# Who copies the values' rows out of PSUM: VectorE behind the keys' maxima, or ScalarE behind their exponentials

## The reference

```
x = x + gnn(xn, edge_attr, src, dst) + mix(xn)          # mix: 4 layers
x = x + ffn(layernorm(x))                                # 16 experts, 2 chosen per node
```

```
q = softmax(split(h @ Wq) * scale, axis=-1)
k = softmax(split(h @ Wk) * scale, axis=-2)              # over the 3125 rows
v = split(h @ Wv)
context = einsum('bhnd,bhne->bhde', k, v)
out = einsum('bhnd,bhde->bhne', q, context) @ Wo + bo
```

## Time and profile before

| what | value |
|---|---|
| median of 3 runs | 2426.01 us (2425.75 to 2429.09) |
| the profiled execution: its time | 2427.93 us |
| the profiled execution: its span | 2426.2 us |
| TensorE matmul busy | 2035.1 us (84%) |
| VectorE busy | 1542.0 us (64%) |
| GpSimd busy | 1365.6 us (56%) |
| ScalarE busy | 951.4 us (39%) |

### The profile page before, as it was taken

One profiled execution on the slowest core, in us unless ns is written; L12 is line 12 of the kernel. 1 busy time (PEld: TensorE's weight loads), 2 busy tenths in 40 slices (PEclk: granted clock), 3 DMA queues, 4 the chain that ended last, 5 costly groups with the idle time before them and its releaser, 6 DMA issues. The chain is left out here.

```text
span 2426.2 us, 36176 instructions
## 1 busy us (share of the span) xinstructions
PE 2035.1 (84%) x10736; PEld 1661.2 (68%) x10736; DVE 1542.0 (64%) x3503; ACT 951.4 (39%) x1978; POOL 1365.6 (56%) x1118
## 2 busy tenths in 40 slices
PE   2359899998989999898999998899999775699990
PEld 2248677777767777776777777777777564688880
DVE  4658777666876767687777667866766456511116
ACT  1234444443544444443444444444444242133330
POOL 4156666667556666665666666566666400366650
PEclk7769999999999999999999999999999786799995
DMA  8652222224222223332322224222222432599997
GB/s 200 187 136 67 73 67 67 67 67 122 64 71 67 69 72 72 96 83 73 72 67 68 68 71 111 68 66 68 67 71 67 88 96 85 181 302 305 306 289 165
DMA packets 269614, 266.96 MB, mean 110 GB/s; under 512 B 146079, under 2 KB 203510, under 8 KB 269526
## 3 DMA queue, kind: packets, MB, share of 16 engines
q0 software_dynamic: 127488, 134.76, 23.2%
q1 hardware_dynamic: 137926, 131.35, 18.6%
q10 hardware_dynamic: 4112, 0.03, 0.1%
HBM read 229.85 MB, written 35.06 MB: 109 GB/s over the span
## 5 line engine op out<-in xcount | busy, mean ns | idle before, releaser
L780 POOL DMA_INDIRECT G<-P_d,src_T x896 | 1159.2, 1294 | 708.4 <-DVE z L419 428.7
L387 ACT ACTIVATE zr<-z 125x512 fp32r<-125x512 f32 x448 | 275.0, 631 | 551.3 <-DVE z L419 507.9
L419 DVE TENSOR_TENSOR z<-bank,G 125x512 f32<-125x512 f32 x448 | 293.4, 686 | 226.9 <-PE bank L379 96.4
L1190 PE MATMUL bank<-TT,W_s 128*128 128x250 f32 (+1 forms) x1280 | 369.3, 439 | 1.0 <-ACT TT L838 0.9
L1057 PE MATMUL bank<-W_s,hid 128*125 128x256 f32 x1600 | 359.6, 379 | 0.0
L1057 PEld LDWEIGHTS bank<-W_s,hid 128*125 128x125 f32 x1600 | 292.8, 187 | 42.8
L1190 PEld LDWEIGHTS bank<-TT,W_s 128*128 128x128 f32 x1280 | 242.7, 196 | 104.3 <-issue 12.1
L393 DVE SCALAR_TENSOR_TENSOR zl<-z,zr 125x512 fp32r<-125x512 f32 x448 | 288.4, 684 | 8.1 <-ACT zr L387 8.1
L371 PE MATMUL bank<-zr,onehot 125*125 125x256 f32 x896 | 271.3, 334 | 12.8 <-DVE zl L393 12.8
L372 PE MATMUL bank<-zl,onehot 125*125 125x256 f32 x896 | 230.3, 288 | 0.0
L922 ACT ACTIVATE hid<-bank,b1c 128x375 f32<-128x375 f32 x320 | 163.0, 521 | 100.1 <-PE bank L1190 90.5
(11 more groups left out here) (310 smaller groups left out, 3103.4 us busy)
## 6 DMA issues: line engine op xcount, KB each, us to landing
W_s<-in_L_ffn_w SPq DMA_DIRECT2D x64, 512.0 KB
hid<-in_L_ffn_w SPq DMA_DIRECT2D x64, 512.0 KB
G<-P_d,src_T POOLq DMA_INDIRECT x896
W_s<-in_L_mix_W SPq DMA_DIRECT2D x8, 1024.0 KB
aT<-attr_d SPq DMA_DIRECT2D x224, 31.2 KB
attr_d<-hn SPq DMA_DIRECT2D x12, 246.1 KB, 3.7
X<-in_x SPq DMA_DIRECT2D x5, 560.0 KB
P_d<-es SPq DMA_DIRECT2D x25, 112.0 KB
```

What stands on the lines that cost most here:

```text
L387: nc.scalar.activation(zr[:, s, k, :], z[:, k, :], ACT.Relu).then_inc(r_done, 1)
L419: nc.vector.tensor_tensor(z[:, k, :], edge_bank[k][0:ET, :], G[:, ST * s + 2 * k:ST * s + 2 * k + 2, :].rearrange("p j d -> p (j d)"), ALU ...
L780: pool.indirect_dma_start(G[:, j, :], None, P_d[:, :], bass.IndirectOffsetOnAxis(ap=src_T[:, at:at + 1], axis=0)).then_inc(g_in[j], 16)
L1190: ins = pe.matmul(to[:, 0:(b - a) * T], W1_s[:, k, part], TT[:, k, TT_PIECES[pc]], start=k == 0, stop=k == KD - 1)
```

## The change

The three copies of the values' rows leave VectorE's program and enter ScalarE's. There they stand behind the two exponentials of their piece: slots 0 and 1 behind those of piece 0, slot 2 behind those of piece 1. They increment the same semaphore `row_dve` as before, and since VectorE also increments it (for the context's update), each copy now waits for its own number in `row_dve` too. Nothing else differs.

```diff
@@ ScalarE, the first pass of a layer @@
                     u0, q0 = l * RING_L + g * RING_GA + (RING_A + LNU), l * (2 * NG) + g * 2
+                    r0 = l * ROW_L + g * ROW_GA + ROW_A
                     for pc, (a, b) in enumerate(PC):
                         act.wait_ge(cd_done, q0 + pc + 1)
                         act.activation(corr[:, pc, :], cdiff[:, pc, :], ACT.Exp).then_inc(corr_done, 1)
                         for h in range(KD):
                             act.activation(eT[:, h, a * T:b * T], RING[(2 * pc + h) % 3][:, 0:(b - a) * T], ACT.Exp,
                                            bias=nb[:, pc, h:h + 1], scale=SCALE).then_inc(ring_act, 1)
+                        for i in ((0, 1), (2,))[pc]:
+                            c, d = RP[i]
+                            act.wait_ge(row_full, r0 + i + 1)
+                            act.wait_ge(row_dve, r0 + i + 1)
+                            act.activation(V5[:, c:d, :, 0:128].rearrange("p j k n -> p (j k) n"),
+                                           ROW[i % 2][0:T, 0:(d - c) * D].rearrange("p (k n) -> p k n", n=128), ACT.Copy).then_inc(row_dve, 1)
                     normalised(u0 + 4, 4)
@@ VectorE, first(g, after) @@
                         dve.tensor_copy(mO[:, :], mN[:, :]).then_inc(m_cp, 1)
-                        for i in ((0, 1), (2,))[pc]:
-                            c, d = RP[i]
-                            dve.wait_ge(row_full, r0 + i + 1)
-                            dve.tensor_copy(V5[:, c:d, :, 0:128].rearrange("p j k n -> p (j k) n"),
-                                            ROW[i % 2][0:T, 0:(d - c) * D].rearrange("p (k n) -> p k n", n=128)).then_inc(row_dve, 1)
                     edges(eg, eg, 0)
```

## The result

Over 13 runs of each, the changed kernel took 2439.12 us (median) and the kernel before 2429.93 us. The two medians lie 9.2 us apart. The ratio over all runs is 1.0034 with a 95% interval of 1.0023 to 1.0044: slower, by 8.3 us (5.6 to 10.7). The forecast was slower by 6.5 us. The forecast was set on the first three of the 13 runs of the kernel before, and the median of all 13 lies 3.9 us above theirs. So its 2432.5 us is to be read as a shift of 6.5, which lies inside the interval. Added to the forecast's 2426.01 us, the measured shift gives 2434.3 us, inside the range of 2428.5 to 2438.5; the 2439.12 us themselves lie 0.6 us above it. The changed kernel, measured again beside later experiments, gave 1.0025 (1.0013 to 1.0036), 6.1 us.

The account below looks back on a forecast made before the run. The prediction took a circle of waits between ScalarE, TensorE and VectorE to bound each group. Sixteen regular groups of 0.31 us and four first groups of 0.38 us add 6.5 us to 2426.01: 2432.5 us, range 2428.5 to 2438.5.

Parts of the forecast that it names:

- The circle: Chain of waits through a 17.00 us regular group, said to set its length; none of VectorE's three copies is in it.
- VectorE's relief: VectorE loses 35.8 us of busy time, costed at nothing: waits of 0.43 us (K3's maximum) and 1.09 us (z) cover it.
- Piece 0: ScalarE's copies behind piece 0's exponentials: TensorE's loads for slot 2 come 0.04 us late, costing nothing that lasts.
- Piece 1, the term that counts: Third copy between last exponential and first TT: 0.50 us step, 0.19 us covered, 0.31 us shift a regular group.
- The first groups: A layer's first group: bank freed 0.21 us late, slot 2 late with it, first TT 0.38 us later.
- The sum: 16 regular groups of 0.31 us and 4 first groups of 0.38 us make 6.5 us: 2432.5 us.
- In series: ScalarE's copy overlaps neither neighbour, or ROW[0] comes so late that slot 2 is late; 2439.4 us; 8 in 100.
- Hidden: Slack behind the first TT takes up the delay, or the copy is short; 2426 to 2429 us; 15 in 100.
- VectorE was the limit: z's start depends on VectorE finishing its third copy; -7.6 us, 2418.4 us; 5 in 100.
- rival E: Repeated run's rival: change costs about 0.5 us a layer at the lower TensorE clock, 2 us or more outside first passes.

Follow-up runs that it names:

- e5: The changed kernel with the third copy executed twice on ScalarE, first into a free buffer; measured +12.6 us (9.2 to 16.0) against the kernel before.
- e6: The kernel before with ScalarE taking the first two es copies between the two zr; measured -1.0 us (-3.2 to 1.2) against it.
- e4: The kernel before with VectorE's three copies cut to one column, values left out of the context; measured +2.4 us (0.2 to 4.4) against it.
- e2: The kernel before with only the copies of slots 0 and 1 moved to ScalarE; measured +0.7 us (-2.2 to 3.4) against it.
- e3: The changed kernel with the third copy placed behind the five es copies on ScalarE; measured +3.6 us (1.5 to 5.8) against the kernel before.
- e1: The kernel before with only the third copy moved to ScalarE, behind piece 1's exponentials; measured +4.9 us (1.7 to 7.8) against it.
- e10: e9 with all three copies on VectorE, slots 0 and 1 behind the normalisations; measured -6.1 us (-8.7 to -3.4) against the kernel before.
- e9: e6 plus zl before the one-hot matrix, hn behind piece 0's update, slots 0 and 1 copied on ScalarE; 2418.02 us, ratio 0.9941 to the kernel before.
- e7: e6 with all three copies on ScalarE, the third behind the es copies; measured -0.2 us (-2.7 to 2.2) against the kernel before.

## Why the prediction was right

**The circle.** It named last exponential, first `TT`, N7, edges' product, z, `zr`, `es`, transposes, context, next keys. e5 shows it at its sharpest: 0.48 us put between the last exponential and the first `TT` make the group 0.49 longer. e6 shows the other end: removing the wait for `es` shortens it.

**VectorE's relief costs at nothing.** Right for this order of the work: e4 takes the copies away without giving them to anyone, and the groups move by 0.01 us. The covers were those named, with 0.42 us left before K3's maximum.

**Piece 0.** A regular group's loads for slot 2 were forecast 0.04 us late, and the rows by form show 1.1 us of such waiting in all, over 20 groups. Right that it doesn't last. In e2 the first groups show 0.10 us of it, which the prediction had only as a part of its 0.38.

**Piece 1, the term that counts.** The start of the copy was forecast at 8.86 us behind the first keys and was there; its duration at 588 ns and measured 597; the start of `TT` at 9.36 us and measured 9.34, because the copy moves the next instruction by 0.48 and not 0.50 us. So 0.29 us a group in place of 0.31. The Trainium skill's cycle count (VectorE: DVE Perf Modes, on the TRN2 errata) gives an estimate of 570 ns for 512 columns. The trace's 597 ns are 27 above it, as the 378 ns for 256 were 21 above; the rows of the trace were the better base. (The 5.8 us that the prediction gives for this price come out at 5.6 with its own overlap of 0.11 us: four times 0.32 and sixteen times 0.27.)

**The first groups.** Forecast 0.38, measured 0.28 us. The step was too dear: I let the 0.21 us of lateness of ROW[0] pass in full to slot 2. TensorE's loads did wait 0.23 us, but the matmuls behind them started 7.84 us behind the first keys as before, since the loads run ahead of the matmuls (in the kernel before they start 0.21 us earlier, at 7.63). N4 came 0.11 us later and the copy at 9.89 us instead of 9.97.

**The sum.** 5.8 us by the groups, 6.5 forecast, 8.3 and 6.1 measured. That the forecast lies so near the second measurement and inside the first one's interval is in part luck: the groups are what it was about, and there it was 0.7 us too high. The traces show where differences arise outside the first passes. Behind the last layer's context the kernel before took 865.8 us to the end of the span, the changed one 872.4, the same changed kernel again 869.0, e2 863.4 and e4 873.9, though all five execute the same instructions there. Over the thirteen comparisons of the table, measured less groups goes from -3.0 to +3.4 us with both signs, so I take the 2.5 us of the first measurement for scatter of the rest; that is argued, not shown. For e3 and e4 the groups' figure lies outside the measured interval, so some of the rest is more than noise of the measurement there. What it is stays open; no run isolates it.

**The rivals.** *In series*: every pair overlapped, and nothing of it came. *Hidden*: excluded by e1, where the third copy alone makes the groups 0.29 us longer, and by e5. *VectorE was the limit*: excluded by e4 for this kernel. The Trainium skill (Perfetto Trace Analysis, on optimizing Scalar and DVE operations) says that offloading from a saturated VectorE may make sense. In this order of the work the trace disagrees; in another it agrees, since between e10 and e9 it is worth 0.18 us a regular group. VectorE's busy share doesn't tell the two apart: 14.43 us of 17.00 in the kernel before, 14.61 of 16.72 in a group of e10. In these runs the sign was whether K3's maximum has to wait for TensorE: it does, by 0.42 us, where the relief was worth nothing, and doesn't in e10.

## What to carry to other kernels

Where engines run in fixed orders, follow the waits around one period of the loop and note each engine's slack at the place where work is put in or taken out; an engine at half load can be the one that has none. Moved work costs its start-to-start distance less the wait that stood there (0.48 - 0.19 = 0.29 us in a regular group), and it is worth looking for a later place, ahead of its reader, where the engine would wait anyway (5 us later in e3). In these runs relief on the other engine paid nothing as long as that engine waited for TensorE behind the relieved place, so test a move again after each reordering: the same two copies on ScalarE were worth nothing (e2), cost 0.12 us (e7) and gained 0.18 us (e9 against e10) a regular group in three orders of the same work.

## What the hardware showed that I had not expected

Eight of the queries' matmuls, early in a layer's second pass, run at either level of TensorE's clock, and which one differs from trace to trace. In the third layer they followed an idle time of 2.74 us in the kernel before and of 3.07 us in the changed one; six microseconds from there on had a granted clock of 1.00 (2.4 GHz) and of 0.72, a mixture of that and 1.2 GHz. The windows view of those six microseconds (length; busy us of PE, PEld, DVE, ACT, POOL; PEclk; DMA), of the kernel before and of the changed one:

```profile
1131.30:1137.30 6.00, 4.50 (x22) 3.46 (x22) 3.30 (x5) 1.27 (x1) 4.28 (x4) 1.00 0.33 84
```

```profile
1134.50:1140.50 6.00, 4.86 (x15) 3.59 (x15) 2.14 (x5) 0.82 (x1) 3.72 (x4) 0.72 0.35 85
```

The eight matmuls took 1.99 and 3.64 us. TensorE's timeline, again of the kernel before and then of the changed one:

```profile
1131.33 1.99 PE L1057 MATMUL bank<-Wq_s,TT 128*125 128x256 f32 x8 [2.74 <-DVE qe L1496]
```

```profile
1134.56 3.64 PE L1064 MATMUL bank<-Wq_s,TT 128*125 128x256 f32 x8 [3.07 <-DVE qe L1498]
```

Over the four layers these eight matmuls took 2.72, 1.99, 1.99 and 1.99 us in the kernel before, 3.64, 1.99, 3.64 and 1.99 in the changed one, and 3.40, 1.99, 3.65 and 2.47 in the changed one again. That is 2.6 and 2.8 us more in sum than in the kernel before, as rival E of the repeated run would have it. The other traces speak against the change as its cause: e1 and e5, which have the third copy too, took only 1.1 and 0.6 us more than the kernel before, while e2 and e4, whose regular groups are those of the kernel before, took 2.4 and 4.6 us more. Over all fourteen traces the sum goes from 8.0 us (e9) to 13.3 (e4), whose matmuls in the third layer were at the same granted clock of 0.72:

```profile
1130.60:1136.60 6.00, 4.46 (x13) 3.34 (x14) 2.55 (x5) 0.60 (x1) 4.70 (x4) 0.72 0.33 85
```

Differences of a few microseconds can thus come and go between traces of kernels that differ elsewhere. The first passes themselves, where the change lies, were at 1.00 in all four layers of both kernels.
